# A three-stage layer on one core: when batch 0 is routed, and where GpSimd issues its rows

## The chip, the cores and the metric

The kernel runs on one core of a Trainium2 chip. The metric is the device time of one execution in microseconds (us); the time of a kernel is the median of several executions. The engines named are TensorE (PE), VectorE (DVE), ScalarE (ACT), GpSimd (POOL) and SyncE (SP), which each work off their own list of instructions in order and wait for each other by semaphores.

## The reference, cut to what matters

`x` is 4 batches of 1024 rows of 128 numbers. Three stages follow each other; the first and the last are the same function with the same weights.

```python
x = x + 0.5 * ffn(layernorm(x))      # 8 experts, each row goes through its best two
x = x + attn(layernorm(x))           # differential attention over the 1024 rows of a batch
x = x + 0.5 * ffn(layernorm(x))

# ffn: logits = t @ Wr.T + br; top_v, top_i = top_k(logits, 2); weights = softmax(top_v)
#      o = relu(t @ W1[e].T + b1[e]) @ W2[e].T + b2[e] for the chosen e;  layer_norm(t + sum(weights * o))
# attn: diff = softmax(q1 @ k1.T * scale) - lam * softmax(q2 @ k2.T * scale)
#       out = diff @ v;  out / rms(out) * 0.2
```

## The kernel before, in words

The first expert pass works on rows sorted by expert, in 78 tiles of 128 rows. Then come four attentions, one for each batch (0 to 3), and then the second expert pass, again 78 tiles. In the code a routing is numbered `a`: 4 to 7 are batches 0 to 3 of the second pass. Routing a batch of the second pass happens inside the attention after next, as its `x` is only finished one attention after its own.

An attention walks over eight query tiles `i` of 128 rows. In the order of each engine's program, for a tile:

- TensorE: the scores of the tile against all keys, two maps of 128 x 1024, as three matmuls each half map (L964 to L966, `scores`); then, two tiles behind, the transposes of the difference (`turn`, L1154) and, three tiles behind, the product with the values (`values`, L1173). The scores of a tile wait until the exponentials have read the two maps of the tile before.
- VectorE: the negated row maxima of both maps (`maxima`, L1841), then the difference of the tile before (`difference`, L1848), then whatever extra the tile has.
- ScalarE: the two exponentials with their row sums (L789), the copy of the turned difference (L766), the copy and squares of the output (L774, L775), then extras.
- GpSimd: `ratio` (L571, L572), which turns the row sums of a tile into the factor that `difference` needs, then extras.

After the last tile of a batch the ends of its turns and values are interleaved with the turn of the next batch's rows (L1106), the product with M (L964 to L966 again) and its copies.

Extras around the change. VectorE in batch 2: sums and statistics of the attention before at tile 3 (`add_values`, L1829, statistics L1338, L1344), and for batch 0: `read_logits` (L1501), `choose` (L1507 to L1518, the two best experts of each row), `place` (L1526 to L1550, each row's slot in the sorted order). Between them TensorE adds `prefix` (L1058, L1059, counts over rows) and ScalarE `gap` (L692). In batch 3 the same is done for batch 1 with the choice at tile 0 and the placing at tile 2, and then `table(0)` (L1560 to L1583): which expert and which rows each tile of the first half (batches 0 and 1) of the second pass has. `table` is a generator with six pieces; `at_once` runs through the pieces it is given.

GpSimd writes the rows of a batch to memory in their sorted places: `scatter(1, b, pieces)` (L499) is one indirect DMA for each of 16 pieces of a batch (eight row tiles, two experts). Piece 0 waits for the slots and for the copied rows. GpSimd's other work in these attentions are `rstd` (L479 to L482, waits for VectorE's statistics) and `value_scale` (L532 to L535), which `add_values` needs.

The second expert pass starts when SyncE has passed `group_ready(0)` (L373 to L377): the table of the first half is ready, the padding rows are written, and all 16 pieces of batch 0 and of batch 1 have landed. It then loads the first tile (L388) and TensorE transposes it (L1069). ScalarE's `make_rows` for batch 2 (in tile 4 of batch 3) reuses batch 0's buffer, so it too waits until batch 0's pieces have landed.

The order of all this is written out by hand, by tile index, in the loops of each engine.

Of the kernel before, what the change touches and what calls it, by code (L numbers as in the profile page):

```python
# [30 lines left out]
def macaron_kernel(nc, x_in, w_q12, w_k12, w_v, lq1, lk1, lq2, lk2, Wr, br, W1, b1, W2, b2, gamma, beta, out):  # L31
    BATCHES, S, D = x_in.shape
# [5 lines left out]
    PAIRS = 2 * TB  # L38
# [21 lines left out]
    with ctx:  # L60
# [263 lines left out]

        def choose_tile(b):

            return 0 if b == BATCHES - 1 else 3

        def place_tile(b):

            return 2 if b == BATCHES - 1 else 5

        def wait_apart(eng, *waits):

# [103 lines left out]
        def _(pool):  # L438
# [136 lines left out]
            for b in range(BATCHES):  # L575
                last, after = b > 0, b < BATCHES - 1
                for i in range(TB):
                    if last and i == 2:
                        value_scale(b - 1, 1)
                    ratio(b, i)  # L580
                    if i == TB - 1:
                        value_scale(b, 0)
                    if b == 0 and i == 1:
                        rstd(BATCHES + 2)
                    if after and i == (2 if b else 4):
                        rstd(n)
                        n += 1
                    if last and i == 3:
                        rstd(n)
                        n += 1  # L590
                    if b < 2 and i == 6:
                        rstd(n)
                        n += 1
                    if b == 0 and i < 5:
                        gather(2, ((4, 5, 6), (7, 8, 9), (10, 11), (12, 13), (14, 15))[i])
                    if b == 0 and i >= 6:
                        gather(3, range(2 * i - 12, 2 * i - 10))
                    if b == 1 and i < 5:
                        gather(3, (range(4, 7), range(7, 10), range(10, 12), range(12, 14), range(14, 16))[i])
                    if b == 2 and i >= 5:  # L600
                        scatter(1, 0, (range(3), range(3, 7), range(7, 10))[i - 5])
                    if b == 3 and i < 2:
                        scatter(1, 0, (range(10, 14), range(14, PAIRS))[i])
                    if b == 3 and 2 <= i < 6:
                        scatter(1, 1, (range(2), range(2, 5), range(5, 9), range(9, 13))[i - 2])
                    if b == 3 and i == TB - 1:
                        scatter(1, 1, range(13, PAIRS))
            assert n == 4 * BATCHES - 1, n
            value_scale(BATCHES - 1, 1)
            scatter(1, BATCHES - 2, range(8))  # L610
# [350 lines left out]
        def _(pe):  # L961
# [214 lines left out]
            def attention(b):  # L1176
                last, after = b > 0, b < BATCHES - 1
                a = BATCHES + b - 1
                for i in range(TB):
                    scores(b, i)  # L1180
                    if b > 1 and i == 0:
                        logits(a - 1)
                    if last and i == 0:
                        turn(b - 1, TB - 1)
                        values(b - 1, TB - 2)
                    if last and i == 1:
                        values(b - 1, TB - 1)
                    if i == 1:
                        multiply_Wv(b)
                    if b > 1 and i == choose_tile(b) + 1:  # L1190
                        prefix(a - 1)
                    if 2 <= i < TB - 1:
                        turn(b, i - 2)
                    if 3 <= i < TB - 1:
                        values(b, i - 3)
                    if last and not after and i == 5:
                        turn_rows(a, 0)
                    if last and not after and i == 6:
                        turn_rows(a, 1)
                turn(b, TB - 3)  # L1200
                if not after:
                    logits(a)
                values(b, TB - 4)
                if after:
                    turn_xn(b + 1)
                    values(b, TB - 3)
                    if last:
                        turn_rows(a, 0)
                    multiply_M(b + 1)
                    turn(b, TB - 2)  # L1210
                    if last:
                        turn_rows(a, 1)
                else:
                    turn(b, TB - 2)
                    values(b, TB - 3)
                    turn(b, TB - 1)
                    values(b, TB - 2)
                    prefix(a)
                    values(b, TB - 1)
# [87 lines left out]
        def _(dve):  # L1307
# [525 lines left out]
            def attention(b, n):  # L1833
# [15 lines left out]

                last, after = b > 0, b < BATCHES - 1  # L1850
                a = BATCHES + b - 1
                for i in range(TB):
                    maxima(i)
                    if i:
                        difference(i - 1)
                    if after and i == TB - 1:
                        xnT_rest(b + 1)
                    if b == 0 and i == 0:
                        at_once(itertools.islice(second_merging, 6))
                    if b == 0 and i == 1:  # L1860
                        at_once(second_merging)
                    if b > 1 and i == 0:
                        read_logits(a - 1)
                    if b > 1 and i == choose_tile(b):
                        at_once(choose(a - 1))
                    if last and i == (0 if after else 1):
                        add_values(b - 1, 0)
                        dve.wait_ge(ln_stats, n)
                        tile_stats(st_r, x_tile(b - 1), halves_of(0))
                    if after and i == (1 if b else 3):  # L1870
                        merge_add(b + 1)
                    if after and i == (2 if b else 4):
                        x_stats(b + 1, n)
                        n += 1
                    if last and i == 3:
                        add_values(b - 1, 1)
                        linked(tile_stats(st_r, x_tile(b - 1), halves_of(1)))
                        batch_stats(st_r, n)
                        n += 1
                    if b < 2 and i == (4 if b else 5):  # L1880
                        dve.wait_ge(ln_stats, n)
                        merge_tiles(b + 2, halves_of(0))
                    if b < 2 and i == 6:
                        linked(merge_tiles(b + 2, halves_of(1)))
                        batch_stats(st_r, n)
                        n += 1
                    if b > 1 and i == place_tile(b):
                        at_once(place(a - 1, b - 2))
                    if b == BATCHES - 1 and i == 4:
                        at_once(table(0))  # L1890
                if after:
                    xm_rest(b + 1)
                difference(TB - 1)
# [153 lines left out]
```

## Time and profile before

| | |
|---|---|
| median of 3 runs | 646.56 us (645.77 to 648.39) |
| the profiled execution | 645.7 us, its span 644.0 us |
| busy PE, PEld | 583.0 us (91%), 537.3 us (83%) |
| busy DVE, ACT, POOL | 452.1 us (70%), 446.4 us (69%), 386.9 us (60%) |
| chain that ended last | PE 56%, DVE 20%, ACT 9%, issue 6%, POOL 6% |
| mean granted TensorE clock | 0.967 of full speed |

The span is the time from the first to the last instruction; the profiled execution's own time is what the runs measure. The chain that ended last follows the last instruction back to what released it, step by step. The four attentions take the time from about 216 to 450 us.

### The profile page before, as it was taken

Reading aid. Unit: us, or ns where it says so; the run is one execution under the profiler, and the core shown is the slowest. Engines: PE = TensorE matmul, PEld = TensorE weight load, DVE = VectorE, ACT = ScalarE, POOL = GpSimd, SP = SyncE. Lnnn points to the kernel's source line nnn. Section 1 sums busy time; section 2 is a strip of 40 time slices with the busy share of each in tenths; the row PEclk is TensorE's granted clock in tenths of the full one; section 3 lists DMA queues with packets and bytes.
Section 4 is the critical chain, followed back from the end, with each engine's and each line's share of the span. In section 5 each row is a group of like instructions: output and inputs, shape, how many; then the busy total and the mean of one; then the engine's idle time right before and its main releaser. Section 6 shows DMA issues by size and latency. Waiting matters only on the chain.

```text
span 644.0 us, 16630 instructions
## 1 busy us (share of the span) xinstructions
PE 583.0 (91%) x4382; PEld 537.3 (83%) x4382; DVE 452.1 (70%) x1421; ACT 446.4 (69%) x1224; POOL 386.9 (60%) x481
## 2 busy tenths in 40 slices
PE   5987999999999788899899899887999999999964
PEld 5887999999999577788797789777989999999831
DVE  5784788446685989699769968976537665467645
ACT  4755666676767577776887696685777777896644
POOL 3007565657667786668515386585775777765633
PEclk9588999999999999899999999999899999999979
DMA  8902233223324210000000001021341423531051
GB/s 259 329 8 58 76 77 71 79 75 89 83 65 80 57 29 17 17 25 18 10 1 0 2 30 36 10 71 31 88 103 57 103 76 97 204 96 40 29 196 66
DMA packets 41882, 45.97 MB, mean 71 GB/s; under 512 B 8726, under 2 KB 32706, under 8 KB 41536
## 3 DMA queue, kind: packets, MB, share of 16 engines
q1 hardware_dynamic: 32496, 27.13, 14.4%
q0 software_dynamic: 9088, 17.75, 10.1%
q8 instruction: 39, 0.64, 0.4%
q14 instruction: 51, 0.42, 0.2%
q10 hardware_dynamic: 208, 0.02, 0.0%
HBM read 25.95 MB, written 19.83 MB: 71 GB/s over the span
## 4 chain that ended last, share of the span: by engine, by line
PE 56%; DVE 20%; ACT 9%; issue 6%; POOL 6%; DMA 1%; ACTq 0%; DVEq 0%; SPq 0%; POOLq 0%
PE banks L1076 20%; PE banks L1086 19%; DVE nb L1841 6%; DVE scratch L1848 3%; PE banks L1069 3%; PE banks L1173 2%; PE banks L964 2%; PE banks L966 2%; PE banks L965 2%; DVE st_r L1338 1%; POOL rows L499 1%; POOL zb L512 1%; DVE mv L1344 1%; ACT tgt L650 1%; POOL rs L480 1%
## 5 line engine op out<-in xcount | busy, mean ns | idle before, releaser
L1076 PE MATMUL banks<-scratch 128*128 128x128 f32 x1248 | 169.1, 279 | 1.8 <-ACT scratch L707 1.3
L1086 PE MATMUL banks<-blocks,scratch 128*128 x1248 | 166.5, 276 | 2.0 <-issue 1.1
L1076 PEld LDWEIGHTS banks<-scratch 128*128 128x128 f32 x1248 | 154.5, 195 | 4.7 <-issue 4.4
L1591 DVE TENSOR_SCALAR scratch<-banks,blocks 128x128 f32<-128x128 f32 x312 | 95.1, 346 | 89.5 <-PE banks L1076 77.5
L1086 PEld LDWEIGHTS banks<-blocks,scratch 128*128 128x128 f32 x1248 | 151.8, 192 | 4.6 <-issue 4.2
L491 POOL DMA_INDIRECT scratch<-xrows,rowbuf x78 | 75.4, 966 | 81.8 <-DVE rowbuf L1486 41.2
L698 ACT ACTIVATE scratch<-banks 128x128 f32<-128x128 f32 x156 | 43.1, 277 | 89.4 <-PE banks L1069 86.9
L789 ACT ACTIVATE scratch<-banks,nb 128x1024 f32<-128x1024 f32 x64 | 71.3, 1115 | 47.6 <-DVE nb L1841 47.2
L524 POOL DMA_INDIRECT results<-scratch,places x78 | 77.8, 998 | 34.4 <-issue 19.7
L714 ACT ACTIVATE scratch<-banks,blocks 128x128 f32<-128x128 f32 x312 | 96.4, 364 | 2.4 <-PE banks L1076 2.1
L707 ACT ACTIVATE scratch<-blocks 128x512 f32 x156 | 97.0, 622 | 0.1
L1841 DVE TENSOR_REDUCE nb<-banks 128x1 f32<-128x1024 f32 x64 | 76.4, 1216 | 10.3 <-PE banks L966 9.0
L499 POOL DMA_INDIRECT rows<-rowbuf,slot x64 | 67.7, 1059 | 26.2 <-issue 15.8
L964 PE MATMUL banks<-xnTh,xmh 128*128 128x512 f32 x128 | 53.4, 417 | 14.1 <-ACT scratch L789 13.6
L1173 PE MATMUL banks<-xn,scratch 128*128 128x128 f32 x512 | 64.8, 281 | 1.3 <-ACT scratch L775 1.3
L1599 DVE TENSOR_TENSOR scratch<-banks,blocks 128x128 f32<-128x128 f32 x156 | 45.0, 288 | 27.4 <-PE banks L1086 19.7
L1173 PEld LDWEIGHTS banks<-xn,scratch 128*128 128x128 f32 x512 | 61.6, 197 | 2.7 <-issue 1.7
L512 POOL DMA_INDIRECT zb<-yrows,slot x48 | 50.4, 1050 | 15.9 <-issue 12.5
L966 PE MATMUL banks<-xnTh,xml 128*128 128x512 f32 x128 | 50.3, 393 | 0.0
L965 PE MATMUL banks<-xnTl,xmh 128*128 128x512 f32 x128 | 50.0, 390 | 0.0
L1069 PE MATMUL banks<-ident,scratch 128*128 128x128 f32 x156 | 43.7, 280 | 6.0 <-DMA scratch<-xrows,rowbuf 4.7
L1848 DVE SCALAR_TENSOR_TENSOR scratch<-scratch,cc 128x1024 f32<-128x1024 f32 x32 | 41.0, 1280 | 5.8 <-POOL cc L572 5.8
(265 smaller groups left out, 896.4 us busy)
## 6 DMA issues: line engine op xcount, KB each, us to landing
scratch<-rows SPq DMA_DIRECT2D x78, 64.5 KB, 1.9
yrows<-scratch SPq DMA_DIRECT2D x78, 64.0 KB, 1.5
scratch<-in_L_ffn_W_dram SPq DMA_DIRECT2D x1, 2048.0 KB, 19.8
xrows<-tgt SPq DMA_DIRECT2D x4, 512.0 KB, 4.2
x<-in_L_attn_x_dram SPq DMA_DIRECT2D x3, 512.0 KB, 8.0
scratch<-xrows,rowbuf POOLq DMA_INDIRECT x78, 2.6
results<-scratch,places POOLq DMA_INDIRECT x78, 2.4
rows<-padrows SPq DMA_DIRECT2D x18, 64.5 KB
```

Source lines behind the costliest of these rows:

```text
L491: pool.indirect_dma_start(xt_v[:, r, 0:D], None, xrows, bass.IndirectOffsetOnAxis(idx[:, T:T + 1], 0)).then_inc(came_or_sent[r], 16)
L499: pool.indirect_dma_start(rows[b // GB], bass.IndirectOffsetOnAxis(slot_v[:, b, j, k:k + 1], 0), rows_of(b)[:, j, k, :], None).then_inc(ro ...
L524: pool.indirect_dma_start(results, bass.IndirectOffsetOnAxis(places[:, q:q + 1], 0), ys[:, r * D:(r + 1) * D], None, bounds_check=2 * N - ...
L707: act.activation(staged(T, 0, FC), blocks[:, bass.ds(at, F)], ACT.Copy).then_inc(w1_sb, 1)
L714: ins = act.activation(hT_of(T, c), hT_at(T, c), ACT.Relu, bias=blocks[:, B1_AT + c:][:, bass.ds(at, 1)], scale=1.0)
L789: act.activation(pp, banks[:, 2 * m * 512:(2 * m + 2) * 512], ACT.Exp, bias=nb[:, 2 * i + m:2 * i + m + 1], scale=1.0, accum_out=ll[:, i:i ...
L964: pe.matmul(o, ah, bh, start=True, stop=False)
L1076: ins = pe.matmul(hT_at(T, c), staged(T, c), xT_of(T), start=True, stop=True)
L1086: ins = pe.matmul(y_at(T), hT_of(T, c), blocks[:, W2_AT + c * D:][:, bass.ds(at, D)], start=(c == 0), stop=(c == FC - 1))
L1173: ins = pe.matmul(bank(6, 0, D), dT[t % 2][:, k * P:(k + 1) * P], vb[:, k * D:(k + 1) * D], start=(k == 0), stop=(k == TB - 1))
L1591: ins = dve.tensor_scalar(hT_of(T, c), hT_at(T, c), blocks[:, B1_AT + c:][:, bass.ds(at, 1)], 0.0, ALU.add, ALU.max)
L1841: dve.tensor_reduce(nb[:, c], banks[:, 2 * m * 512:(2 * m + 2) * 512], AX_X, ALU.max, negate=True).then_inc(nb_ready, 1)
```

## The change

Three things are moved. In batch 2, the choice for batch 0 goes from tile 3 to tile 4, and the placing from tile 5 to tile 6; ScalarE's `gap` and TensorE's `prefix` follow `choose_tile` (from tile 4 to tile 5), and the prefix now stands behind the tile's turn and values in TensorE's order instead of ahead of them. In batch 3 `choose_tile` and `place_tile` stay; its prefix is in tile 1, where no turn or values(b, ...) of the same batch stand, so its order stays too. The table of the first half, formerly all at tile 4 of batch 3, is spread over tiles 4 to 7 with 2, 2, 1 and the last piece. The pieces of batches 0 and 1 are issued in other tiles:

| batch of attention, tile | 2,5 | 2,6 | 2,7 | 3,0 | 3,1 | 3,2 | 3,3 | 3,4 | 3,5 | 3,6 | 3,7 |
|---|---|---|---|---|---|---|---|---|---|---|---|
| before | 3 | 4 | 3 | 4 | 2 | 2 | 3 | 4 | 4 | 0 | 3 |
| after | 0 | 2 | 7 | 3 | 4 | 0 | 4 | 4 | 4 | 0 | 4 |

Up to tile 1 of batch 3 they are batch 0's, from tile 2 on batch 1's.

```diff
@@ -324,11 +324,11 @@
 
         def choose_tile(b):
 
-            return 0 if b == BATCHES - 1 else 3
+            return 0 if b == BATCHES - 1 else 4
 
         def place_tile(b):
 
-            return 2 if b == BATCHES - 1 else 5
+            return 2 if b == BATCHES - 1 else 6
 
         def wait_apart(eng, *waits):
 
@@ -597,14 +597,14 @@
                         gather(3, range(2 * i - 12, 2 * i - 10))
                     if b == 1 and i < 5:
                         gather(3, (range(4, 7), range(7, 10), range(10, 12), range(12, 14), range(14, 16))[i])
-                    if b == 2 and i >= 5:
-                        scatter(1, 0, (range(3), range(3, 7), range(7, 10))[i - 5])
+                    if b == 2 and i >= 6:
+                        scatter(1, 0, (range(2), range(2, 9))[i - 6])
                     if b == 3 and i < 2:
-                        scatter(1, 0, (range(10, 14), range(14, PAIRS))[i])
-                    if b == 3 and 2 <= i < 6:
-                        scatter(1, 1, (range(2), range(2, 5), range(5, 9), range(9, 13))[i - 2])
+                        scatter(1, 0, (range(9, 12), range(12, PAIRS))[i])
+                    if b == 3 and 3 <= i < 6:
+                        scatter(1, 1, (range(4), range(4, 8), range(8, 12))[i - 3])
                     if b == 3 and i == TB - 1:
-                        scatter(1, 1, range(13, PAIRS))
+                        scatter(1, 1, range(12, PAIRS))
             assert n == 4 * BATCHES - 1, n
             value_scale(BATCHES - 1, 1)
             scatter(1, BATCHES - 2, range(8))
@@ -1187,12 +1187,12 @@
                         values(b - 1, TB - 1)
                     if i == 1:
                         multiply_Wv(b)
-                    if b > 1 and i == choose_tile(b) + 1:
-                        prefix(a - 1)
                     if 2 <= i < TB - 1:
                         turn(b, i - 2)
                     if 3 <= i < TB - 1:
                         values(b, i - 3)
+                    if b > 1 and i == choose_tile(b) + 1:
+                        prefix(a - 1)
                     if last and not after and i == 5:
                         turn_rows(a, 0)
                     if last and not after and i == 6:
@@ -1849,6 +1849,7 @@
 
                 last, after = b > 0, b < BATCHES - 1
                 a = BATCHES + b - 1
+                tabling = table(0)
                 for i in range(TB):
                     maxima(i)
                     if i:
@@ -1886,8 +1887,8 @@
                         n += 1
                     if b > 1 and i == place_tile(b):
                         at_once(place(a - 1, b - 2))
-                    if b == BATCHES - 1 and i == 4:
-                        at_once(table(0))
+                    if b == BATCHES - 1 and i >= 4:
+                        at_once(itertools.islice(tabling, (2, 2, 1, 2)[i - 4]))
                 if after:
                     xm_rest(b + 1)
                 difference(TB - 1)
```

## Rows read from the trace of the kernel before

**Rows 1.** The chain of waits, 425 to 475 us: start, us, what.
```profile
444.13 2.30 DMA rows<-rowbuf,slot
```

**Rows 2.** Timeline of TensorE, end of batch 3: start us, us, what, [idle before, releaser].
```profile
438.30 1.09 PE L1154 MATMUL banks<-ident,scratch 128*128 128x128 f32 x8 [0.56 <-DVE scratch L1848]
...
446.19 0.43 PE L1058 MATMUL banks<-cnt,upper 128*128 128x64 f32 x2 [2.27 <-DVE cnt L1517]
...
450.62 0.48 PE L1069 MATMUL banks<-ident,scratch 128*128 128x128 f32 x1 [0.76 <-DMA scratch<-rows]
```

**Rows 3.** Timeline of GpSimd, batch 3.
```profile
404.96 0.54 POOL L571 TENSOR_TENSOR cc<-l,minus 128x1 f32<-128x1 f32 x1 [1.19 <-ACT scratch L789]
...
414.35 0.27 POOL L479 TENSOR_SCALAR rs<-mv 128x8 f32<-128x8 f32 x1 [1.68 <-DVE mv L1344]
...
419.56 0.96 POOL L499 DMA_INDIRECT rows<-rowbuf,slot  x1 [0.31 <-issue]
...
421.82 0.59 POOL L571 TENSOR_TENSOR cc<-l,minus 128x1 f32<-128x1 f32 x1
...
430.01 2.09 POOL L499 DMA_INDIRECT rows<-rowbuf,slot  x1 [0.16 <-ACT scratch L789]
```

**Rows 4.** Timeline of VectorE, batch 3.
```profile
410.09 1.32 DVE L1848 SCALAR_TENSOR_TENSOR scratch<-scratch,cc 128x1024 f32<-128x1024 f32 x1
...
414.07 2.32 DVE L1841 TENSOR_REDUCE nb<-banks 128x1 f32<-128x1024 f32 x2
...
417.50 0.20 DVE L1560 CAST carry_i<-carry 128x8 int32<-128x8 f32 x1
...
418.66 0.47 DVE L1570 TENSOR_TENSOR zb<-sidx,tend 1x312 f32<-1x312 f32 x1
...
421.89 2.35 DVE L1841 TENSOR_REDUCE nb<-banks 128x1 f32<-128x1024 f32 x2
...
429.88 1.28 DVE L1848 SCALAR_TENSOR_TENSOR scratch<-scratch,cc 128x1024 f32<-128x1024 f32 x1 [1.18 <-POOL cc L572]
```

**Rows 5.** Timeline of VectorE, batch 2.
```profile
351.56 0.28 DVE L1507 TENSOR_REDUCE m<-lg 128x8 f32<-128x64 f32 x1
...
355.08 1.13 DVE L1829 SCALAR_TENSOR_TENSOR x<-scratch,so,x 128x128 f32<-128x128 f32 x4
...
357.82 2.32 DVE L1841 TENSOR_REDUCE nb<-banks 128x1 f32<-128x1024 f32 x2
...
361.99 2.59 DVE L1841 TENSOR_REDUCE nb<-banks 128x1 f32<-128x1024 f32 x2 [0.66 <-PE banks L966]
...
365.69 0.18 DVE L1526 COPY rowbuf<-dest 128x16 int32<-128x16 int32 x1
...
368.91 2.35 DVE L1841 TENSOR_REDUCE nb<-banks 128x1 f32<-128x1024 f32 x2
...
373.11 2.59 DVE L1841 TENSOR_REDUCE nb<-banks 128x1 f32<-128x1024 f32 x2 [0.66 <-PE banks L966]
```

**Rows 6.** Timeline of TensorE, batch 2.
```profile
355.14 0.43 PE L1058 MATMUL banks<-cnt,upper 128*128 128x64 f32 x2 [1.48 <-DVE cnt L1517]
...
360.30 0.50 PE L964 MATMUL banks<-xnTh,xmh 128*128 128x512 f32 x1 [1.84 <-ACT scratch L789]
...
365.74 0.48 PE L964 MATMUL banks<-xnTh,xmh 128*128 128x512 f32 x1
...
371.42 0.50 PE L964 MATMUL banks<-xnTh,xmh 128*128 128x512 f32 x1
```

**Rows 7.** Timeline of ScalarE, batch 2.
```profile
359.05 1.11 ACT L789 ACTIVATE scratch<-banks,nb 128x1024 f32<-128x1024 f32 x1 [4.49 <-DVE nb L1841]
...
375.25 1.11 ACT L789 ACTIVATE scratch<-banks,nb 128x1024 f32<-128x1024 f32 x1
```

**Rows 8.** Windows, 440 to 456: us, busy PE, PEld, DVE, ACT, POOL, PEclk, DMA.
```profile
447.00:448.00 1.00, 1.00 (x11) 1.00 (x10) 0.90 (x6) 0.00 (x0) 0.00 (x0) 0.87 0.00 0
...
454.00:455.00 1.00, 1.00 (x8) 1.00 (x8) 0.00 (x0) 0.89 (x3) 0.69 (x2) 0.71 0.33 46
```

## The prediction

> **What bounds the kernel now.** I read the chain of waits first, then the timelines of GpSimd, VectorE, TensorE and ScalarE over the last two attentions (batches 2 and 3), and the windows with the granted clock. Below, "maxima 4" is L1841 of query tile 4, "scores" L964 to L966, "difference" L1848, "ratio" L571 with L572, "an issue" one L499. The change touches only the stretch from 350 to 450 us. Behind it stands the second expert pass, started by one event: its first tile is transposed at 450.62 behind a load of rows from memory, which had to wait until the last issue of batch 1 (444.13) had landed at 444.13 + 2.30 = 446.43 [rows 1]. TensorE sat 0.76 us for it, its attention being over [rows 2]. So the start of the last 193 us is set by GpSimd.
>
> Followed back on GpSimd, that last issue belongs to an unbroken chain: from the statistics of tile 3 of batch 3 (rstd at 414.35) it is not idle again for more than the gap of 0.3 between issues [rows 3]. In it lie rstd, 3 issues, ratio 4, 4 issues, ratio 5, 4 issues, ratios 6 and 7, the value scale, 3 issues. VectorE feels it: difference 5 waited 1.18 us for the ratio [rows 4]. Whatever VectorE and TensorE gain in tiles 4 to 7 is given back while this chain is as long; only its start and its number of issues count.
>
> **Part 1, the choice of batch 0 moved from tile 3 to tile 4 of batch 2 (and its prefix, exponential and placing with it).** Before, choose ran 351.56 to 355.08, 3.52 us, in front of the sums and statistics of tile 3, so maxima 4 came at 357.82 although its scores were long done [rows 5]; TensorE waited 1.48 us in front of the prefix and 1.84 in front of scores 5 [rows 6]. After:
> - maxima 4 starts at 357.82 - 3.52 = 354.30. Scores 5 follow 2.48 us behind (357.82 to 360.30): 356.78. TensorE would be free at 360.30 - 1.48 - 1.84 - 0.5 (the prefix, an estimate from its 0.43 us row) = 356.5, so the maxima decide.
> - Maxima, difference: 3.43 us (414.07 to 417.50 [rows 4]), so 357.73; then choose, 3.52: maxima 5 at 361.25 and scores 6 at 363.73. TensorE's own pace (360.30 to 365.74 without idle is 5.44 a tile) with the prefix behind the values gives 356.78 + 5.44 + 0.5 = 362.7; no wait for the prefix, since counts are ready at 361.2. Before, scores 6 began at 365.74: 2.0 earlier, 1.5 already paid back.
> - Maxima 6 come 1.69 behind scores 6 (371.42 to 373.11): 365.42. Then 3.70 (361.99 to 365.69, maxima that had waited for scores, and a difference) and the placing, 3.22 (365.69 to 368.91): maxima 7 at 372.34, against 373.11.
> - The exponential of tile 7 follows 1.23 behind (357.82 to 359.05 [rows 7]): 373.6. Before it ran at 375.25 without idle in front of it: ScalarE was the late one there, and by the same count it is free at about 373.1. What ends the attention (this exponential, the transpose's copy, then the turn of the next batch's rows) hangs on it: 1.6 us earlier.
> Batch 3 so begins 1.6 us earlier; the stages between the attentions are a chain of TensorE, ScalarE and VectorE with nothing of GpSimd in it. Bounds: 0, if something I don't see in tile 7 or behind it holds the end (rival D), and 3.3, the two idle stretches of TensorE. I take 1.6, which is what the recurrence gives.
>
> **Part 2, GpSimd's rows of batch 0.** 10 in batch 2 (3, 4, 3 in tiles 5 to 7) become 9 (2, 7 in tiles 6 and 7); 6 in batch 3 become 7 (3, 4). One issue costs 0.96 + 0.31 = 1.27 us [rows 3]. Ahead of ratio 2 of batch 3 the stretch from tile 7 on then holds 14 issues, 9 before: 5 x 1.27 = 6.4 us more. Queued behind them: ratios 0 to 2, both value scales, and VectorE's differences, with TensorE's turns behind those. Ratio 2 ran at 404.96 after a wait of 1.19, and was used by the difference at 410.09 [rows 3, 4], 4.2 us after it ended. At worst 6.4 - 1.2 - 4.2 = 1.0 us sticks out; but the seven issues fall in the stretch between the attentions, GpSimd has other gaps there, and its ratio 7 of batch 2 no longer has four issues ahead. I take 0, with 1.0 as the upper end. Nothing waits for batch 0's rows early: the next user is the row making in tile 4.
>
> **Part 3, rows of batch 1.** 2, 3, 4, 4 in tiles 2 to 5 and 3 in tile 7 become 0, 4, 4, 4 and 4. The two of tile 2 were ahead of the wait for statistics (414.35, after 1.68 us idle), so their going saves nothing on the chain. Inside the chain stand 16 issues instead of 14: 2 x 1.27 = **2.54 us more**, one of them in front of ratio 4, one in front of the landing. No issue stands in tile 6 before or after.
>
> **Part 4, the first table in four parts.** In one piece it held VectorE 417.50 to 421.89, 4.39 us, in front of maxima 5; its first two parts end at about 418.7, so maxima 5 come 3.2 us earlier still [rows 4]. Nothing of this reaches the end: GpSimd's chain now starts at 414.35 - 1.6 = 412.75, so ratio 4, which ran at 421.82, runs at 421.82 - 1.6 + 1.27 = 421.5 and ends at 422.5, while VectorE has come through maxima 5 at about 419.3 and waits 3 us. Differences 5 and 6 stand where they stood within 0.4 us. The parts in tiles 5 and 6 lie in this waiting; the last (0.8 us, an estimate from the 3.2 us that the four parts behind the first two take) sits between differences 6 and 7, where it delays difference 7 by some 0.3 us, off the chain. The table is ready some 17 us later, at about 439, still ahead of the landing at 447. Were GpSimd not late, this part would be worth up to 3.2 us; I take 0.
>
> **How long an issue is.** The issue at 430.01 took 2.09 us, beside the difference that started at 429.88; others take 0.96 [rows 3, 4]. The Trainium skill (GPSIMD Engine Reference, section 1, Specifications) says that GpSimd's memory interfaces are shared with VectorE and contend with VectorE instructions that have two SBUF inputs, which the difference has. By that rule difference 4, now released by the ratio, meets the next issue as difference 5 did, the number of long issues in the chain stays two, and the sum stands; if such meetings are chance, one is gone and the sum is 1.0 lower (rival B).
>
> **The sum.** -1.6 (start of the chain) + 2.54 (two issues) = +0.9 us at the landing, and so at the start of the second pass. From there every stage is paced by its own steps, and the shift is carried to the end. The profiled execution took 645.7 us (span 644.0 and 1.7 around it): 646.6. It lies 0.9 under the median 646.56 of the runs, whose 0.9 I add back: **647.5 us**. From no change this kernel can tell about 0.5%, 3.2 us, so the forecast is "no measurable change".
>
> **Rivals.**
> - **A, the two added issues are hidden** and the earlier start remains: 646.56 - 1.6 = 645.0. It needs slack on GpSimd between 414 and 441; for it speaks only the shortness of each issue, against it the unbroken row of [rows 3].
> - **B, one long issue fewer:** 647.5 - 1.0 = 646.5.
> - **C, slower, by TensorE's clock.** After idling 2.27 us at 446.19 [rows 2] TensorE's granted clock fell within 447 to 448 to half and came back within 454 to 455 [rows 8], so prefix, last values and the first expert tiles ran at 1.2 GHz. After the change TensorE has finished the values of tile 4 by about 435.5 and difference 6 is not there before 438: 2.5 us of idle, where the turn at 438.30 had waited 0.56 [rows 2]. If the clock falls behind this one as well and stays low, the 5.4 us of turns and values up to 443.9 take twice that; the prefix then starts at about 449.3, the first expert tile at 450.6 + 3.1, and half a microsecond more runs slow there: +3.6, **650.2**. It decides from the point where the half clock begins ahead of 440. Against it: the waits of 1.84 and 1.48 in batch 2 brought no fall, and an early fall can also mean an early return. The Trainium skill (TensorE: Matmul & The Clock Gate, The HAM clock gate) has the slow clock as the default that activity releases, which agrees with the order of fall and return here; no term uses it.
> - **D, part 1 brings nothing:** the full 2.54 stays: 649.1. For it: VectorE's choose is only moved by one tile. Against: tile 4 of batch 2 has no other extra work, so one tile's overload becomes use of another's slack.
>
> **Chances.** Forecast 0.52 (own range 646 to 649), A 0.12, B 0.10, C 0.12, D 0.14. Faster by over 0.5% needs under 643.3, which no case gives, only the scatter of A: 0.04. Slower by over 0.5% is over 649.8: most of C and a tail of D: 0.10. The rest, 0.86, is within. The range goes from just below A, 644.6, to C, 650.3.
>
> **What would show it.** In the changed profile: no wait of TensorE in front of the prefix of batch 2; scores 5 of batch 2 near 356.8; batch 3's first scores some 1.6 earlier; rstd of tile 3 at about 412.8; maxima 5 at about 417; difference 4 waiting some 3 us for the ratio; ratio 4 near 421.5; four issues behind the value scale, the last landing near 447.4; the first expert transpose near 451.5. The prediction is wrong if ratio 4 comes well before 421, if batch 3 starts unchanged, if a ratio of tiles 0 to 2 holds up its difference, or if the clock's low stretch is not one but two.

## The result and the profile after

Before 645.5 us (median of 22 runs), changed 649.0 (22 runs). The ratio, changed over before, is 1.0038, 95% interval 1.0028 to 1.0048: 2.4 us slower (1.8 to 3.1). The two medians lie 3.5 apart; I go by the ratio and its interval. That is inside the 0.5% that was called no change in advance, and 1.5 us more than the +0.9 forecast; but the interval leaves out 1, so it is a small slowdown and not none. The profiled execution of the changed kernel has a span of 647.7 us against 644.0.

Two points in time do most of the work below. **t0** is the start of the merge in tile 1 of batch 2 (L1647), a point that the change can't reach; it is at 339.48 before and at 341.17 changed, so 1.69 us of the difference between these two single profiles have nothing to do with it (the first expert transpose of the whole program is already 1.5 apart, 50.7 and 52.2; from 10 to 50 us the mean granted clock is 0.74 before and 0.70 changed). **T** is the expert transpose of the second pass that waits for a load (L1069), counted from t0.

Changed kernel, VectorE, batch 2 and 3 (start us, us, what, [idle before, releaser]), the answer to [rows 4, 5]:

```profile
341.17 1.41 DVE L1647 TENSOR_TENSOR scratch<-scratch,gammab 128x512 f32<-128x512 f32 x2
...
356.00 2.33 DVE L1841 TENSOR_REDUCE nb<-banks 128x1 f32<-128x1024 f32 x2
...
374.06 2.35 DVE L1841 TENSOR_REDUCE nb<-banks 128x1 f32<-128x1024 f32 x2
...
418.70 2.36 DVE L1841 TENSOR_REDUCE nb<-banks 128x1 f32<-128x1024 f32 x2
424.58 1.28 DVE L1848 SCALAR_TENSOR_TENSOR scratch<-scratch,cc 128x1024 f32<-128x1024 f32 x1 [3.53 <-POOL cc L572]
```

TensorE, batch 2 and the end of batch 3, to [rows 6, 2]:

```profile
358.48 0.50 PE L964 MATMUL banks<-xnTh,xmh 128*128 128x512 f32 x1 [0.47 <-ACT scratch L789]
...
364.01 0.33 PE L1058 MATMUL banks<-cnt,upper 128*128 128x64 f32 x2
...
365.46 0.50 PE L964 MATMUL banks<-xnTh,xmh 128*128 128x512 f32 x1 [0.89 <-ACT scratch L789]
...
440.13 1.09 PE L1154 MATMUL banks<-ident,scratch 128*128 128x128 f32 x8 [2.35 <-DVE scratch L1848]
...
448.04 0.43 PE L1058 MATMUL banks<-cnt,upper 128*128 128x64 f32 x2 [2.29 <-DVE cnt L1517]
...
452.50 0.45 PE L1069 MATMUL banks<-ident,scratch 128*128 128x128 f32 x1 [1.07 <-issue]
453.73 0.48 PE L1069 MATMUL banks<-ident,scratch 128*128 128x128 f32 x1 [0.78 <-DMA scratch<-rows]
```

GpSimd, batch 3, to [rows 3]:

```profile
406.59 0.53 POOL L571 TENSOR_TENSOR cc<-l,minus 128x1 f32<-128x1 f32 x1
...
414.40 0.27 POOL L479 TENSOR_SCALAR rs<-mv 128x8 f32<-128x8 f32 x1 [1.57 <-DVE mv L1344]
...
418.59 1.10 POOL L499 DMA_INDIRECT rows<-rowbuf,slot  x1 [0.56 <-issue]
...
423.51 0.59 POOL L571 TENSOR_TENSOR cc<-l,minus 128x1 f32<-128x1 f32 x1
...
424.72 2.08 POOL L499 DMA_INDIRECT rows<-rowbuf,slot  x1 [0.17 <-issue]
...
447.23 0.96 POOL L499 DMA_INDIRECT rows<-rowbuf,slot  x1 [0.30 <-issue]
```

Taken from t0, everything up to GpSimd's chain is earlier by what was counted: rstd of tile 3 stands at 414.40 - 341.17 = 73.23 after t0, before at 414.35 - 339.48 = 74.87, 1.64 earlier. From rstd to the last issue it takes 32.83 us (414.40 to 447.23) instead of 29.78 (414.35 to 444.13): 3.05 later. So T is 112.56 (453.73 - 341.17) against 111.14 (450.62 - 339.48): +1.42. The two spans lie 3.8 us apart before rounding; the rest of that is 1.69 ahead of t0 and 0.66 behind T (194.0 us to the end against 193.3).

Windows of the changed kernel (us, busy PE, PEld, DVE, ACT, POOL, PEclk, DMA, GB/s), to [rows 8]:

```profile
449.00:450.00 1.00, 1.00 (x9) 1.00 (x9) 0.88 (x5) 0.00 (x0) 0.00 (x0) 0.72 0.00 0
...
459.00:460.00 1.00, 1.00 (x8) 1.00 (x7) 0.95 (x4) 0.02 (x1) 0.69 (x2) 0.66 0.58 127
```

TensorE's clock falls to half within 449 to 450 and is back within 459 to 460, some 10 us; before it was low from within 447 to 448 to within 454 to 455, some 7. The second transpose, at T, is 6.0 us ahead of the clock's return (453.73 to 459.7), before 4.0 (450.62 to 454.6).

### The profile page after: what moved, and what is told of

It reads as the page before. It is cut to its first block, busy times and chain, and to the rows that moved or that the text cites. A ratio compares the mean times of both kernels' runs of the same rounds, so it can differ in the third digit from the quotient of the medians.

```text
span 647.7 us, 16633 instructions
## 1 busy us (share of the span) xinstructions
PE 586.8 (91%) x4382; PEld 540.9 (83%) x4382; DVE 451.7 (70%) x1421; ACT 447.0 (69%) x1224; POOL 386.3 (60%) x481
## 4 chain that ended last, share of the span: by engine, by line
PE 59%; DVE 18%; POOL 8%; ACT 7%; issue 6%; DMA 1%; ACTq 0%; SPq 0%; POOLq 0%; DVEq 0%
PE banks L1076 21%; PE banks L1086 20%; DVE nb L1841 5%; DVE scratch L1848 3%; POOL rows L499 3%; PE banks L1069 3%; PE banks L1173 2%; PE banks L964 2%; PE banks L966 2%; PE banks L965 2%; DVE st_r L1338 1%; POOL zb L512 1%; PE banks L992 1%; PE banks L1012 1%; DVE mv L1344 1%
## 5 line engine op out<-in xcount | busy, mean ns | idle before, releaser
L499 POOL DMA_INDIRECT rows<-rowbuf,slot x64 | 66.2, 1035 | 24.2 <-issue 16.7
L1069 PE MATMUL banks<-ident,scratch 128*128 128x128 f32 x156 | 43.6, 279 | 7.0 <-DMA scratch<-xrows,rowbuf 4.6
L571 POOL TENSOR_TENSOR cc<-l,minus 128x1 f32<-128x1 f32 x32 | 19.7, 616 | 48.0 <-ACT scratch L789 47.7
```

What stands on the lines that cost most here:

```text
L499: pool.indirect_dma_start(rows[b // GB], bass.IndirectOffsetOnAxis(slot_v[:, b, j, k:k + 1], 0), rows_of(b)[:, j, k, :], None).then_inc(ro ...
```

## The experiments

The kernels ran in four groups, each beside runs of the kernel before on the same chip. On the chips of experiments 1 to 4, 9 to 11 and 12 the kernel before takes 773 us, on that of 5 to 8 646. The added time lies in the two expert passes, so I read the stretch from t0 to T. No kernel was profiled on both kinds of chip, but experiment 11 is the kernel before up to its last few us of attention: both have rstd at 74.87 and the last issue at 104.65 after t0. There is one profile of each kernel. The ratios are each against the kernel before on the same chip; the changed kernel itself did not run again beside the experiments.

**1. Only the choice's move and batch 0's rows.**

```diff
 # changed kernel, with
-                    if b == 3 and 3 <= i < 6:
-                        scatter(1, 1, (range(4), range(4, 8), range(8, 12))[i - 3])
-                    if b == 3 and i == TB - 1:
-                        scatter(1, 1, range(12, PAIRS))
+                    if b == 3 and 2 <= i < 6:
+                        scatter(1, 1, (range(2), range(2, 5), range(5, 9), range(9, 13))[i - 2])
+                    if b == 3 and i == TB - 1:
+                        scatter(1, 1, range(13, PAIRS))
...
-                    if b == BATCHES - 1 and i >= 4:
-                        at_once(itertools.islice(tabling, (2, 2, 1, 2)[i - 4]))
+                    if b == BATCHES - 1 and i == 4:
+                        at_once(tabling)
```

> The changed kernel with the table in one piece at tile 4 and batch 1's rows issued as before (2, 3, 4, 4 in tiles 2 to 5, 3 in tile 7): only the choice's move and batch 0's rows are left. I measure D, from the scores of tile 3 of batch 2 to the first expert transpose of the second pass: 105.8 us before (344.80 to 450.62), 107.2 changed (346.49 to 453.73). Theory G (GpSimd's chain sets the start, the choice's move is worth 1.6): D = 104.2, the time 1.6 below before, ratio 0.9975. Rival D (the move brings nothing, the whole loss is less than two issues): D = 105.8, ratio 1.000. Rival Q (batch 0's seven issues between the attentions hold something up): D over 106.

Timelines of VectorE, GpSimd and TensorE of this kernel:

```profile
408.76 1.41 DVE L1647 TENSOR_TENSOR scratch<-scratch,gammab 128x512 f32<-128x512 f32 x2
...
481.92 0.27 POOL L479 TENSOR_SCALAR rs<-mv 128x8 f32<-128x8 f32 x1 [1.01 <-DVE mv L1344]
...
511.69 0.96 POOL L499 DMA_INDIRECT rows<-rowbuf,slot  x1 [0.30 <-issue]
...
518.17 0.45 PE L1069 MATMUL banks<-ident,scratch 128*128 128x128 f32 x1 [0.67 <-DMA scratch<-rows]
```

T = 518.17 - 408.76 = 109.41, 1.73 under the kernel before (in D, which the expectations use, it is 5.3 less; they differ by the constant way from t0 to the scores of tile 3). Rstd at 73.16, and from there to the last issue 29.77, the 29.78 of before. So the choice's move is worth 1.6 to 1.7 us, and the seven issues between the attentions hold up nothing. Ratio 0.9977 (0.9948 to 1.0006): in the right place, too wide to stand alone.

**2. The table back in one piece**, all else as changed (of the diff above only its second part, on `tabling`).

> The changed kernel with the table in one piece at tile 4; everything else as changed. G: VectorE waits for the ratio anyway, so the table's place is worth nothing: D = 107.2 within 0.3, VectorE's wait in front of difference 4 falls from 3.5 us to about 0.3. Rival T (the parts, the last one between differences 6 and 7, cost or save): D off 107.2 by 0.5 or more.

```profile
409.98 1.41 DVE L1647 TENSOR_TENSOR scratch<-scratch,gammab 128x512 f32<-128x512 f32 x2
...
493.49 1.29 DVE L1848 SCALAR_TENSOR_TENSOR scratch<-scratch,cc 128x1024 f32<-128x1024 f32 x1 [0.58 <-POOL cc L572]
...
522.55 0.33 PE L1069 MATMUL banks<-ident,scratch 128*128 128x128 f32 x1 [0.84 <-DMA scratch<-rows]
```

T = 112.57, changed 112.56. VectorE's wait in front of difference 4 shrinks from 3.53 to 0.58, as the table now fills it, and nothing else moves: the difference starts at 83.51 after t0, changed at 83.41. Ratio 1.000 (0.997 to 1.003), which can't resolve 1.4 us on this chip.

**3. Only batch 1's rows**, on the kernel before.

```diff
 # kernel before, with
-                    if b == 3 and 2 <= i < 6:
-                        scatter(1, 1, (range(2), range(2, 5), range(5, 9), range(9, 13))[i - 2])
+                    if b == 3 and 3 <= i < 6:
+                        scatter(1, 1, (range(4), range(4, 8), range(8, 12))[i - 3])
                     if b == 3 and i == TB - 1:
-                        scatter(1, 1, range(13, PAIRS))
+                        scatter(1, 1, range(12, PAIRS))
```

> The kernel before with only batch 1's rows issued as changed (0, 4, 4, 4 in tiles 2 to 5, 4 in tile 7). G: two issues of 1.27 us and the two waits ahead of piece 0 (0.4) now inside the chain: D = 105.8 + 3.0 = 108.8, ratio 1.0045 or more, the slowest of the four. Rival D: no more than the changed kernel, D = 107.2.

```profile
408.90 1.41 DVE L1647 TENSOR_TENSOR scratch<-scratch,gammab 128x512 f32<-128x512 f32 x2
...
523.06 0.33 PE L1069 MATMUL banks<-ident,scratch 128*128 128x128 f32 x1 [0.95 <-DMA scratch<-rows]
```

T = 114.16, 3.02 over before. Ratio 1.0048 (1.0020 to 1.0077), the slowest of the four. Experiments 1 and 3 add up: -1.73 + 3.02 = +1.29, against +1.42 for the whole change.

**4. Batch 1's rows as before, the table in four parts** (of the diff of experiment 1 only its first part, on `scatter`).

> The changed kernel, table in four parts, but batch 1's rows issued as before (2, 3, 4, 4, 3). G: D = 104.2, the same as with the table in one piece, since the chain from the statistics of tile 3 to the last landing is that of the kernel before, begun 1.6 earlier. Rival T: off that by 0.5 or more, up to 3.2 faster if VectorE's table were what held tiles 5 to 7.

```profile
409.54 1.41 DVE L1647 TENSOR_TENSOR scratch<-scratch,gammab 128x512 f32<-128x512 f32 x2
...
519.16 0.33 PE L1069 MATMUL banks<-ident,scratch 128*128 128x128 f32 x1 [0.97 <-DMA scratch<-rows]
```

T = 519.16 - 409.54 = 109.62, against 109.41 with the table in one piece: the parts bring nothing. The 0.2 that they cost lie for the most part in the first two issues behind ratio 4, 2.09 and 0.99 us here, 1.06 and 1.87 in experiment 1. Ratio 0.9967 (0.9943 to 0.9992): the change without its third part is faster than before.

**5. The two waits ahead of piece 0 taken in tile 2.**

```diff
-            def scatter(p, b, pieces=range(2 * TB)):
+            def scatter(p, b, pieces=range(2 * TB), waits=True):
...
-                if pieces[0] == 0:
+                if pieces[0] == 0 and waits:
                     wait_apart(pool, (slots_ready, GB + b + 1), (rows_copied, b + 1))
...
+                    if b == 3 and i == 2:
+                        wait_apart(pool, (slots_ready, GB + 2), (rows_copied, 2))
                     if b == 3 and 3 <= i < 6:
-                        scatter(1, 1, (range(4), range(4, 8), range(8, 12))[i - 3])
+                        scatter(1, 1, (range(4), range(4, 8), range(8, 12))[i - 3], False)
```

> The changed kernel with the two waits that stand ahead of piece 0 of batch 1 (slots ready, rows copied) taken by GpSimd at tile 2, where it waits anyway, instead of behind rstd of tile 3. Theory W: in the changed kernel these waits cost 0.4 us inside GpSimd's chain (0.56 us from rstd to the first issue, where 0.18 stood before), the part of the loss that two issues don't explain. Then the first issue follows rstd by 0.2 us and T, from the merge of tile 1 of batch 2 (L1647) to the first expert transpose that waits for the load, is 112.56 - 0.4 = 112.2. Rival: the 0.4 comes back elsewhere (a longer issue beside a difference), T = 112.5.

```profile
413.02 0.27 POOL L479 TENSOR_SCALAR rs<-mv 128x8 f32<-128x8 f32 x1 [1.57 <-DVE mv L1346]
...
416.82 1.10 POOL L499 DMA_INDIRECT rows<-rowbuf,slot  x1 [0.17 <-issue]
...
452.06 0.47 PE L1071 MATMUL banks<-ident,scratch 128*128 128x128 f32 x1 [0.88 <-DMA scratch<-rows]
```

t0 is at 339.80. The first issue follows rstd's last step by 0.17 instead of 0.56 and T = 112.26, 0.30 less. Both waits had long been fulfilled: in tile 2 they delay nothing (ratio 3 starts 70.50 after t0, changed 70.51). Behind rstd they cost 0.4 us of GpSimd's own time, of which 0.3 reach the second pass. Ratio 1.0025 (1.0010 to 1.0040).

TensorE's clock in this kernel, by the windows:

```profile
450.00:451.00 1.00, 0.12 (x1) 0.14 (x1) 0.00 (x0) 0.00 (x0) 0.92 (x2) 1.00 0.26 57
451.00:452.00 1.00, 0.18 (x1) 0.00 (x0) 0.00 (x0) 0.79 (x3) 0.80 (x2) 0.72 0.27 66
```

It held through the wait of 2.27 us in front of the prefix (446.27) and fell within 451 to 452, in the idle time of the second pass's first tile: counted from t0 some 3.4 us later than in the changed kernel (111.6 against 108.3).

**6. TensorE kept busy at the end of the last attention** (changed kernel).

```diff
+            def keep_busy(n):
+
+                pe.wait_ge(p_ready, 2 * TB * BATCHES)
+                for _ in range(n):
+                    pe.transpose(bank(1, 0, P), ident[:, :], ident[:, :])
...
                     values(b, TB - 2)
+                    keep_busy(16)
                     prefix(a)
                     values(b, TB - 1)
+                    keep_busy(16)
```

> The changed kernel with 16 transposes of the unit matrix into a bank that nobody reads in front of the prefix of batch 2's routing and 16 more behind the last values: added work that fills TensorE's two waits at the end of the last attention. Theory C (part of the loss, about 1 us, is the longer low stretch of TensorE's clock, 10.2 us where the kernel before had 6.8, which began behind the wait of 2.3 us): the low stretch shrinks or goes, T stays 112.6 (GpSimd's chain is untouched), and the time falls by 1 to 3 us against the changed kernel: ratio to before 0.999 to 1.001. Rival: the clock is noise of that one profile or falls all the same; ratio 1.003 as the changed kernel.

Windows of this kernel over the same stretch:

```profile
444.00:448.00 4.00, 3.45 (x31) 3.21 (x30) 3.41 (x18) 0.88 (x7) 0.96 (x1) 1.00 0.10 33
448.00:452.00 4.00, 2.82 (x23) 2.26 (x20) 0.49 (x3) 1.96 (x9) 3.02 (x6) 1.00 0.24 57
452.00:456.00 4.00, 3.90 (x36) 3.71 (x34) 2.56 (x9) 3.28 (x12) 3.09 (x4) 1.00 0.41 108
```

PEclk stays at 1.00. T = 112.45 (450.67 - 338.22), as changed, and from T to the end it takes 192.1 us (span 642.8 - 450.67) instead of 194.0 (this profiled execution, 644.5, is 1.9 under the median of its own runs, so I go by the medians). Ratio 1.0008 (0.9992 to 1.0024), against 1.0025 of experiment 5 in the same group, which has the same T within 0.2: medians 646.4 and 647.6. More work on TensorE, and the median is about 1 us lower; the two intervals overlap, and experiment 5 only stands in for the changed kernel here.

**7. Fewer rows behind rstd**, eleven issues instead of sixteen; the plus lines take the place of the changed kernel's two calls for batch 1's rows.

```diff
+                    if b == 3 and i == 3:
+                        scatter(1, 1, range(4, 5))        # ahead of rstd(n)
...
+                    if b == 3 and 2 <= i:
+                        scatter(1, 1, (range(4), range(5, 7), range(7, 10), range(10, 13), range(13, 14), range(14, PAIRS))[i - 2])
```

> The changed kernel with batch 1's rows issued 4 in tile 2, 1 in tile 3 ahead of rstd, then 2, 3, 3, 1, 2 in tiles 3 to 7: 11 issues behind rstd instead of 16, one of them in a wait of GpSimd. G: the chain loses 5 issues, 6.4 us, until something else holds: ScalarE's exponential of tile 7 and TensorE's own pace of about 5.9 us a tile, which I count to a first expert transpose at T = 106.4 to 107.6, against 112.56 changed and 111.14 before. The time falls by 3.5 to 4.5 us against before: ratio 0.993 to 0.995. Rival D (VectorE and TensorE bound tiles 4 to 7 after all): T not under 110.

```profile
415.42 0.26 POOL L479 TENSOR_SCALAR rs<-mv 128x8 f32<-128x8 f32 x1
...
445.35 0.63 PE L1058 MATMUL banks<-cnt,upper 128*128 128x64 f32 x2 [3.09 <-DVE cnt L1517]
...
449.31 0.27 PE L1069 MATMUL banks<-ident,scratch 128*128 128x128 f32 x1
450.36 0.30 PE L1069 MATMUL banks<-ident,scratch 128*128 128x128 f32 x1 [0.77 <-ACT scratch L698]
```

Windows of this kernel:

```profile
444.00:448.00 4.00, 2.65 (x12) 2.65 (x13) 3.29 (x17) 0.21 (x1) 0.00 (x0) 0.68 0.08 18
448.00:452.00 4.00, 2.92 (x21) 2.55 (x20) 0.93 (x4) 2.29 (x10) 1.61 (x4) 0.89 0.22 50
452.00:456.00 4.00, 4.00 (x36) 3.85 (x35) 2.95 (x11) 3.12 (x12) 2.99 (x4) 1.00 0.30 83
```

A miss in size. The second transpose is at T = 450.36 - 340.46 = 109.90, where 106.4 to 107.6 was expected, all but at the 110 of the expectation's rival D. It is no longer behind a load but behind ScalarE's copy: the attention's own end on TensorE (prefix, then the last values) is the bound. And rstd stands at 74.96 after t0 instead of 73.23, now without idle ahead of it: five issues ahead of it are more than GpSimd's gap holds. The low clock is over by about 448.9, ahead of the first transpose (449.31), and yet it takes 194.1 us from T to the end (span 644.4), as long as in the changed kernel. Ratio 0.9991 (0.9978 to 1.0004).

**8. The same with the filling transposes** of experiment 6.

> The former kernel with the 16 and 16 filling transposes as well. If both theories hold and add up: T as in the former kernel plus at most 1 us, since the attention's own end on TensorE is then near the bound and the fillers stand in its order, and the second pass begins at full clock: 1 to 2 us under the former kernel. Rival: fillers delay the prefix and the last values by their own length, up to 2 to 3 us, and nothing is gained.

```profile
444.00:456.00 12.00, 11.23 (x97) 10.71 (x97) 7.55 (x33) 6.93 (x27) 7.48 (x10) 1.00 0.32 82
```

The clock (the column behind POOL) stays at 1.00 from 444 to 456. T = 109.72, ratio 0.9982 (0.9969 to 0.9995), medians 644.5 against 645.5: the median is 1 us lower here too, at the lower end of what was expected, with overlapping intervals. In the profile of experiment 7 the second pass begins at full clock already, so there the clock at its start can't be what the fillers bring.

**9 and 10. Rows 4 in tile 2, then 2, 3, 3, 1, 3; values ahead of the prefix**, with and without fillers (8 and 16).

```diff
+                    if b == 3 and 2 <= i:
+                        scatter(1, 1, (range(4), range(4, 6), range(6, 9), range(9, 12), range(12, 13), range(13, PAIRS))[i - 2])
...
-                    prefix(a)
                     values(b, TB - 1)
+                    keep_busy(8)       # experiment 9 only
+                    prefix(a)
+                    keep_busy(16)      # experiment 9 only
```

> The changed kernel with batch 1's rows 4 in tile 2, none ahead of rstd, then 2, 3, 3, 1, 3 in tiles 3 to 7 (12 behind rstd, its start not held up), the last values of TensorE in front of the prefix instead of behind it, and filling transposes, 8 in front of the prefix and 16 behind. In the kernel with 11 behind rstd and 5 ahead, rstd came 1.7 us late and TensorE's end, not the rows, set the start. G: the first expert transpose comes 3 us behind the last landing again, at T1 = 106.6 (before 109.9, changed 111.3), the second pass at full clock takes 193.3 from there (before 194.5): 4.5 us below before, ratio 0.993. Rival: TensorE's end or ScalarE's copies still hold it, T1 = 108 to 109, ratio 0.996 to 0.998.

> The former kernel without the filling transposes. Theory C: T1 the same, but TensorE now idles some 5 us before the second pass with only the prefix in it, its clock is at half there, and the pass takes 194.5 to 196 from T1: 1.3 to 3 us above the former kernel, ratio 0.995 to 0.998. Rival (the clock's stretch is not governed by this idle): no difference from the former kernel.

The first expert transpose of 9, and the same of 10:

```profile
519.57 0.27 PE L1073 MATMUL banks<-ident,scratch 128*128 128x128 f32 x1
```

```profile
516.12 0.30 PE L1067 MATMUL banks<-ident,scratch 128*128 128x128 f32 x1 [1.95 <-issue]
```

With t0 at 412.16 and 409.24, T1, the first expert transpose from t0, is 107.41 with fillers and 106.88 without, before 109.94; ratios 0.9932 (0.9903 to 0.9961) and 0.9950 (0.9926 to 0.9975). Both miss the 106.6 expected, by 0.8 and 0.3. The second transposes lie 0.1 apart (T = 108.14 and 108.05); from there the rest takes 250.7 and 251.8 us. The order is as theory C has it, but the intervals overlap.

**11. The kernel before with the fillers** of experiment 6.

> The kernel before with the 16 and 16 filling transposes around the prefix and last values, nothing else. C: T1 = 110 as before plus at most 0.3 (its slack in front of the load is 0.8), no low stretch at the start of the second pass, 193.3 us from there instead of 194.5: ratio 0.998. Rival: the fillers' length (1.7 us each) shows in T1 and the ratio is 1.000 or above.

T1 = 110.80, 0.86 later, ratio 1.0017 (0.9989 to 1.0044): the rival. In the kernel before, TensorE's end lies close to the load, so the fillers behind the values delay the start; the granted clock was 1.00 from 516 to 524, and whether that saves as much stays below the noise of this chip.

**12. Three rows in tile 2 instead of four**, then 3, 3, 3, 1, 3, with 8 fillers ahead of the prefix as in experiment 9 and 12 behind it.

> The kernel with values ahead of the prefix and fillers, with 3 of batch 1's rows in tile 2 and then 3, 3, 3, 1, 3, and 12 filling transposes instead of 16 behind the prefix. There, rstd of tile 3 came at 74.8 after the merge of tile 1 instead of 73.2, since four issues and ratio 3 stood ahead, and the first expert transpose at 107.4 (106.9 without fillers). G: rstd at 73.2 again, 1.6 earlier, one issue of 1.27 more behind it, so the landing 0.3 earlier: T1 = 106.6, no low clock at the start of the second pass, ratio to before 0.993. Rival: the fourth issue in tile 2 was not what held rstd, rstd stays at 74.8 and T1 grows by 1.3.

Rstd's third step, L481, and the issue behind it on GpSimd, in experiment 12 and then in 9:

```profile
484.45 0.27 POOL L479 TENSOR_SCALAR rs<-mv 128x8 f32<-128x8 f32 x1
...
486.56 0.93 POOL L481 TENSOR_TENSOR nm<-mv,rs 128x8 f32<-128x8 f32 x1
...
487.95 1.10 POOL L499 DMA_INDIRECT rows<-rowbuf,slot  x1 [0.17 <-issue]
```

```profile
486.95 0.27 POOL L479 TENSOR_SCALAR rs<-mv 128x8 f32<-128x8 f32 x1
...
489.05 0.20 POOL L481 TENSOR_TENSOR nm<-mv,rs 128x8 f32<-128x8 f32 x1
...
489.72 1.10 POOL L499 DMA_INDIRECT rows<-rowbuf,slot  x1 [0.17 <-issue]
```

Half a miss: with t0 at 410.92, rstd is at 73.53, close to the 73.2 expected (74.79 in experiment 9), but T1 = 107.84, not 106.6. Thirteen issues stand behind rstd instead of twelve, which takes back the 1.26 us of the earlier start, and L481 meets VectorE's difference (486.11): 0.93 us where 0.20 stand in experiment 9. So the last issue is at 102.44, in experiment 9 at 101.65. Ratio 0.9970 (0.9947 to 0.9994).

## Why the prediction was right

**What bounds the kernel.** Right: GpSimd's chain from rstd of tile 3 to the last landing. Experiments 1 and 3 move the second pass by what they do to that chain's start and length; VectorE's 3.53 us wait for ratio 4 is the "some 3 us" that was forecast. One reading was wrong. The transpose at 450.62 is the pass's second, and the 0.76 us ahead of it is not TensorE's wait for the pass to start. From the kernel before, TensorE:

```profile
446.68 2.75 PE L1173 MATMUL banks<-xn,scratch 128*128 128x128 f32 x16
449.42 0.45 PE L1069 MATMUL banks<-ident,scratch 128*128 128x128 f32 x1
```

The first transpose is at 449.42, 3.0 us behind the landing, and follows the last values without idle time. So in the kernel before TensorE's own end, at half clock, was as late as the load, and the start had two bounds side by side. It did no harm to the sum: added rows make the load the later one (the first transpose then waits, 1.07 us changed, 0.69 in experiment 3), and T1 shifts like T (109.94 to 111.33). It does tell why taking rows away brings so little (experiment 7).

**Part 1, -1.6.** Right, step by step. With the 1.69 taken off, maxima 4 are at 354.31 (forecast 354.30), scores 5 at 356.79 (356.78), scores 6 at 363.77 (363.73), maxima 7 at 372.37 (372.34), and the prefix of batch 2 has no wait. Rstd comes 1.64 earlier. Rival D falls with experiment 1.

**Part 2, 0.** Right: ratio 2 ends at 407.6, its difference runs at 410.18 without a wait.

**Part 3, +2.54.** The mechanism was right, the size was off: 3.05 from rstd to the last issue, 3.02 at T in experiment 3. Of the missing 0.5, 0.4 are the two waits ahead of piece 0: 0.56 us ahead of the first issue, 0.17 without them (experiment 5). The prediction had noted that the waits exist and that batch 1's first two issues leave tile 2, but not that the waits move into the chain with them. The four issues behind ratio 4 take 0.13 more in sum (the long one 2.08 instead of 1.86, the one beside it 0.98 instead of 1.07), which is the rest. Rival A falls.

**Part 4, 0.** Right (experiments 2 and 4).

**How long an issue is.** The issue behind ratio 4 took 2.08 us beside the difference at 424.58, as the shared interface named in the Trainium skill (GPSIMD Engine Reference, section 1, Specifications) would have it, and the one behind ratio 5 took 2.09 in every profile of which I read this stretch. The two long issues of the chain stayed two, as the sum had it, and rival B falls. It does not hold for every meeting. In the kernel before an issue started 0.06 us behind the difference of 410.09 [rows 4] and took no longer than usual:

```profile
410.15 0.96 POOL L499 DMA_INDIRECT rows<-rowbuf,slot  x1 [0.30 <-issue]
```

**The sum.** +0.94 was forecast at the start of the second pass and +1.42 measured. "From there every stage is paced by its own steps, and the shift is carried to the end" is the step that failed a little: 0.66 more in the profiles, and some 1.0 more by the ratio (2.4 - 1.4; with the ratio's interval 0.4 to 1.7). The cause of this rest is not shown. Behind T the changed kernel spends 2.0 us more at half clock, which would be worth 1.0 (an estimate: half of that time). For it speaks that fillers hold PEclk at 1.00 there and the medians are 1 us lower. Against it speak the profiles without fillers: from T to the clock's return and from T to the end it is 4.0 and 193.3 us before, 6.0 and 194.0 changed, 6.2 and 195.0 in experiment 5, but 0 and 194.1 in experiment 7, whose fillers in experiment 8 then lowered the median all the same. The clock also differs elsewhere: over the last 34 us of the span its mean is 0.87 before, 0.85 changed, 0.89 in experiment 7, but 0.82 and 0.81 with the fillers of experiments 6 and 8. The absolute forecast, 647.5, started from a median of 3 runs that lay 1.05 above that of the 22; the 649.0 measured is at the edge of its own range of 646 to 649.

**Rival C** had the right place and the wrong way. TensorE did idle 2.35 us in front of the turn at 440.13, where 2.5 was said, and its clock did not fall behind it. It fell behind the second wait (2.29 us) as before, and only came back later. What decides when it falls stays open: experiment 5 has the same two waits (2.37 and 2.27 us) and a fall that is some 3.4 us later.

## What to carry to other kernels

When an engine works off an unbroken row from some event to a landing that starts the next stage, count everything that stands in that row, the waits that are already fulfilled too (0.2 us each here), and move work to the idle time ahead of the event; spreading another engine's work while it waits for that row is worth nothing (experiments 2 and 4). Move too much ahead, and the event itself comes late (experiment 7, by 1.7 us), and look for the next bound close behind: there it was TensorE's own end. Best here was experiment 9, the rows early, the last values ahead of the prefix and TensorE kept busy up to the next stage: 0.993 (0.990 to 0.996) of the kernel before. Without the fillers it was 0.995 (0.993 to 0.998), so the fillers' part is not shown.

## What the runs showed of the hardware

- The same kernel takes 646 us on one chip and 773 on others, while rstd and the last issue stand where they stood, 74.87 and 104.65 after t0 (kernel before and experiment 11). In experiment 1 TensorE stood still once for 15.6 us in the second pass behind a copy of ScalarE, which itself waited 22.4 us for something outside what the profile of this core shows. What that is stays open.
- With transposes whose output nobody reads TensorE's clock stayed at 2.4 GHz around the start of the second pass, where it had gone down to 1.2 for 6.8 us (experiment 5) and 3.4 us (experiment 7). The median was 1 us lower in both pairs (646.4 against 647.6, 644.5 against 645.5), with overlapping intervals.
- A small GpSimd operation can take five to six times as long beside VectorE: the product of eight values per row in rstd (L481) takes 0.20 us in experiment 9, and with a difference beside it 0.93 in experiment 12 and 1.23 in the changed kernel and in the one before.
